# Cross-attention on one core: GpSimd's input split and output scale-and-shift cut into single instructions, with other work between the halves

## The chip, the cores and the metric

The kernel runs on one core of one Trainium2 chip. A time is device microseconds (us) of one execution. Five engines each work through a list of their own: TensorE (PE: matmuls), VectorE (DVE), ScalarE (ACT), GpSimd (POOL) and SyncE (SP), which here issues nearly all DMAs. They meet only at semaphores.

## The reference

```python
Q = (q @ Wq + bq); K = (k @ Wk + bk); V = (v @ Wv + bv)     # q = x, k = v = ctx; 16 heads of 64
scores = einsum('bhqd,bhkd->bhqk', Q, K) / 8 * mask
ctx = einsum('bhqk,bhkd->bhqd', softmax(scores), V)
x = q + ctx @ Wo + bo
return (x - mean(x)) * rsqrt(var(x) + 1e-5) * gamma + beta
```

The batch has 16 items, each with 512 queries, 512 keys and width 512; all is float32.

## The kernel before

Each float32 operand of a large matmul is carried as two float16 parts, a rounded one and the difference that is left ("split"), so that a product takes three matmuls. ScalarE rounds, and VectorE takes the difference, for Q, K, V, the probabilities and the context; for the inputs x and ctx it is GpSimd that takes it. All differences of probabilities are VectorE's already (`split_probs`, L933), in both kernels.

A batch item has 8 pairs of heads. A pair has 4 query tiles of 128 rows and two heads, so 8 score tiles of 128x512. A tile goes: TensorE `scores` (L436) into one of 4 PSUM banks; VectorE `mask_and_max` (L919) masks and takes the row maxima; GpSimd `negate_max` (L1228) negates the maxima of two tiles; ScalarE `exponentials` (L608) writes `probs` and frees the bank; GpSimd `scale_sums` (L1234) scales the row sums of four tiles; VectorE `invert_sums` (L927) inverts them; ScalarE `round_probs` (L622) and VectorE `split_probs` (L933) make the two parts; SP issues a transposing DMA (L275), and TensorE `values` (L457) multiplies by V. `probs` has 8 buffers, so an exponential waits for the `split_probs` of the same tile of the pair before.

The projections ("fills", L383 to L385) and the output projection share three PSUM banks. After the output projection of item n: VectorE adds (L962) and takes statistics, GpSimd `deviation` (L1244 to L1252) makes the scale and shift of the layer norm, ScalarE `standardize` (L638) applies them, and GpSimd `scale_and_shift` multiplies by gamma (L1258) and adds beta (L1260) for each of four row tiles of 128x512. Each second instruction waits for the first. SP `store` (L265) waits for the result.

For the next item, ScalarE `round_input` (L576) rounds a 128x512 tile of x or ctx; then GpSimd `split_input` scales the raw tile (L1208) and subtracts the rounded part (L1211). The Q fill of the next item waits for all four tiles of x, its K fill for all four of ctx.

Each engine's `body(prev, here, nxt, first)` is an order written out by hand for a software pipeline over batch items: `here` is the item whose pairs 2 to 7 run, `nxt` the item whose inputs are prepared and whose pairs 0, 1 and a part of 2 start at the end of the body, and `prev` the one whose output is normalized. `batches` calls it once with only `nxt`, once for item 0, then in a hardware loop for items 1 to 14 (a "pass" below), and twice to finish. In a list an instruction that waits holds back all that is behind it. SP's list at the end of a body has: transpose of pair 0's query tile 0 of `nxt`, `store` of `prev`'s tiles 0 to 2, load of `acc` tile 0, transpose of query tile 1, `store` of tile 3.

Of the kernel before, what the change touches and what calls it, by code (L numbers as in the profile page):

```python
# [41 lines left out]
def cross_attention(nc, x, xt, ct, mask, wq, bq, wk, bk, wv, bv, wo, bo, gamma, beta, out):  # L42
    ctx = ExitStack()
    with ctx:
# [142 lines left out]
        def out_no(n, q):  # L187
            return n * QT + q + 1
# [17 lines left out]
        def raw_input(t, i):  # L206
            return raw[:, "xc".index(t), i, :]
# [988 lines left out]
        def _(pool):  # L1196
# [27 lines left out]
            def negate_max(n, p, queries):  # L1224
                for q in queries:
                    wait_alone(pool, masked, tile_no(n, p, 2 * q + 1))
                    cut = slice(2 * q, 2 * q + 2)
                    nc.gpsimd.tensor_scalar(neg_max[:, p % 2, cut], row_max[:, p % 2, cut], -1.0, 1.0, ALU.mult,  # L1228
                                            ALU.mult).then_inc(max_negated, 1)
# [21 lines left out]
                pool.wait_ge(rstd_done, n + 1)  # L1251
                nc.gpsimd.tensor_tensor(shift, neg_mean, rstd, ALU.mult).then_inc(shift_done, 1)  # L1252

            def scale_and_shift(n, tiles):
                for q in tiles:
                    i = out_no(n, q)
                    pool.wait_ge(centered, i)
                    nc.gpsimd.tensor_tensor(acc[:, q, :], acc[:, q, :], gamma_b[:, :], ALU.mult).then_inc(scaled, 1)  # L1258
                    pool.wait_ge(scaled, i)
                    nc.gpsimd.tensor_tensor(acc[:, q, :], acc[:, q, :], beta_b[:, :], ALU.add).then_inc(normed, 1)  # L1260

            def body(prev, here, nxt, first):
                if here is not None:
                    scale_sums(here, 2, 0)
                if prev is not None:
                    add_bo(prev, range(1, 2))
                if here is not None:
                    negate_max(here, 2, range(2, 4))
                    scale_sums(here, 2, 1)
                    negate_max(here, 3, range(0, 2))  # L1270
                    scale_sums(here, 3, 0)
                if prev is not None:
                    add_bo(prev, range(2, 4))
                if here is not None:
# [12 lines left out]
                if prev is not None:  # L1287
                    scale_and_shift(prev, range(0, 1))
                if here is not None:
                    negate_max(here, 5, range(2, 4))  # L1290
                    scale_sums(here, 5, 1)
                if nxt is not None:
                    split_input(nxt, "x", range(0, 1))
                if here is not None:
                    negate_max(here, 6, range(0, 1))
                if nxt is not None:
                    split_input(nxt, "x", range(1, 2))
                    scale_biases(nxt)
                if here is not None:
                    negate_max(here, 6, range(1, 2))  # L1300
                if nxt is not None:
                    split_input(nxt, "x", range(2, 3))
                if here is not None:
                    scale_sums(here, 6, 0)
                    negate_max(here, 6, range(2, 3))
                if nxt is not None:
                    split_input(nxt, "x", range(3, 4))
                if here is not None:
                    negate_max(here, 6, range(3, 4))
                if nxt is not None:  # L1310
                    split_input(nxt, "c", range(0, 1))
                if here is not None:
                    scale_sums(here, 6, 1)
                if nxt is not None:
                    split_input(nxt, "c", range(1, 2))
                if here is not None:
                    negate_max(here, 7, range(0, 2))
                if nxt is not None:
                    split_input(nxt, "c", range(2, 4))
                if here is not None:  # L1320
                    scale_sums(here, 7, 0)
                    negate_max(here, 7, range(2, 4))
                    scale_sums(here, 7, 1)
                if prev is not None:
                    scale_and_shift(prev, range(1, 3))
                if nxt is not None:
                    negate_max(nxt, 0, range(0, 2))
                    scale_sums(nxt, 0, 0)
                    negate_max(nxt, 0, range(2, 4))
                    scale_sums(nxt, 0, 1)  # L1330
                    negate_max(nxt, 1, range(0, 1))
                if prev is not None:
                    scale_and_shift(prev, range(3, 4))
                if nxt is not None:
                    negate_max(nxt, 1, range(1, 2))
                    scale_sums(nxt, 1, 0)
                    negate_max(nxt, 1, range(2, 4))
# [33 lines left out]
```

## Time and profile before

| | us |
|---|---|
| median of 3 runs | 2435.55 (2431.52 to 2437.57) |
| profiled execution, its own time | 2432.53 |
| its span, first to last instruction | 2430.7 |
| PE busy | 2206.0 (91%) |
| DVE busy | 2099.9 (86%) |
| ACT busy | 1790.6 (74%) |
| POOL busy | 824.3 (34%) |

A pass of the hardware loop takes about 146.5 us; the rows below are of one of them (here = item 6; VectorE branches back at 968 us and at 1115 us), and the others repeat it closely. Busy shares are averages, so what counts is who waits for whom in each stretch.

### The profile page before, as it was taken

The page shows a single profiled execution, that of the slowest core. Times are in us where ns is not written, and L with a number is a line of the kernel's source. Part 1 is how long each engine was busy: PE and PEld are TensorE (multiplying, and loading weights), DVE is VectorE, ACT ScalarE, POOL GpSimd, SP SyncE. Part 2 cuts the span into 40 slices and gives each one's busy share as a digit, 9 for nine tenths or more (in the row PEclk, how much of TensorE's full clock was granted, in tenths as well). Part 3 has the DMA queues.
Part 4 walks back from the last instruction along what each step waited for, and adds up shares of the span by engine and source line. Part 5 has one row for each costly group of instructions (what it writes and reads, how often), then busy time and mean ns, then how long its engine had stood idle before and what let it go on. Part 6 is the DMA issues. An engine that isn't in the chain of part 4 may idle for free.

```text
span 2430.7 us, 45821 instructions
## 1 busy us (share of the span) xinstructions
PE 2206.0 (91%) x12348; PEld 897.6 (37%) x12348; DVE 2099.9 (86%) x4411; ACT 1790.6 (74%) x3809; POOL 824.3 (34%) x1320
## 2 busy tenths in 40 slices
PE   3789999999999899999989999999999999999995
PEld 1234433334333343333334333343333334333342
DVE  6799988979889898888989889798888979889893
ACT  3688786867868687786877858687786867859782
POOL 2023252423425243242423415143242422415324
PEclk9899999999999999999999999999999999999997
DMA  5378887677767868677687777868677687767774
GB/s 203 74 149 158 164 148 160 130 169 144 159 143 148 179 125 179 133 146 166 130 172 144 155 148 147 172 127 177 135 143 169 125 175 143 151 141 148 158 134 109
DMA packets 1117592, 363.26 MB, mean 149 GB/s; under 512 B 1073504, under 2 KB 1073504, under 8 KB 1117408
## 3 DMA queue, kind: packets, MB, share of 16 engines
q1 hardware_dynamic: 1114288, 361.58, 72.7%
q14 instruction: 165, 1.35, 0.2%
q10 hardware_dynamic: 3120, 0.01, 0.1%
q8 instruction: 19, 0.31, 0.0%
HBM read 76.30 MB, written 16.78 MB: 38 GB/s over the span
## 4 chain that ended last, share of the span: by engine, by line
PE 51%; issue 16%; ACT 11%; DVE 11%; POOL 8%; DMA 1%; DVEq 1%; ACTq 1%; POOLq 0%; SPq 0%
PE fill_ps L383 12%; PE fill_ps L384 11%; PE fill_ps L385 11%; PE score_ps L436 9%; PE ctx_ps L457 6%; ACT probs L608 5%; DVE p L933 4%; DVE score_ps L919 3%; ACT p L622 2%; POOL acc L1258 2%; ACT v L587 2%; POOL raw L1208 2%; POOL neg_max L1228 2%; POOL acc L1260 1%; DVE row_max L919 1%
## 5 line engine op out<-in xcount | busy, mean ns | idle before, releaser
L608 ACT ACTIVATE probs<-score_ps,neg_max 128x512 f32<-128x512 f32 x1024 | 694.4, 685 | 312.4 <-POOL neg_max L1228 272.2
L933 DVE SCALAR_TENSOR_TENSOR p<-probs,inv_sum,p 128x512 f16<-128x512 f32 x1024 | 851.8, 872 | 1.8 <-ACT p L622 1.8
L919 DVE CUSTOM_DVE_ANT_0 score_ps<-score_ps,mask_sb,small 128x512 f32<-128x512 f32 x1024 | 728.1, 751 | 46.6 <-PE score_ps L436 41.0
L622 ACT ACTIVATE p<-probs,inv_sum 128x512 f16<-128x512 f32 x1024 | 681.8, 724 | 79.4 <-DVE inv_sum L927 75.9
L436 PE MATMUL score_ps<-k,q 64*128 64x512 f16 x3072 | 457.1, 389 | 106.0 <-ACT probs L608 104.0
L1228 POOL TENSOR_SCALAR neg_max<-row_max 128x2 f32<-128x2 f32 x512 | 176.6, 346 | 1040.3 <-DVE row_max L919 1039.0
L457 PE MATMUL ctx_ps<-pT,v 128*64 128x512 f16 x3072 | 361.3, 385 | 17.9 <-DMA pT<-p 11.8
L436 PEld LDWEIGHTS score_ps<-k,q 64*128 64x128 f16 x3072 | 139.1, 95 | 397.4 <-ACT probs L608 240.5
L457 PEld LDWEIGHTS ctx_ps<-pT,v 128*64 128x64 f16 x3072 | 166.3, 111 | 207.0 <-issue 63.4
L383 PE MATMUL fill_ps<-cT,wk 128*128 128x512 f16 x512 | 202.7, 396 | 26.0 <-DVE k L948 24.9
L1234 POOL TENSOR_SCALAR down_sum<-row_sum 128x4 f32<-128x4 f32 x256 | 75.3, 294 | 398.3 <-ACT probs L608 390.6
L383 PE MATMUL fill_ps<-wv,cT 128*128 128x512 f16 x512 | 199.7, 390 | 6.5 <-DVE v L954 6.5
L608 ACT ACTIVATION_READ_ACCUMULATOR probs<-score_ps,neg_max 128x1 f32 x1024 | 205.2, 200 | 0.0
L383 PE MATMUL fill_ps<-xT,wq 128*128 128x512 f16 x512 | 196.9, 385 | 5.2 <-POOL xT L1211 5.2
L384 PE MATMUL fill_ps<-cT,wk 128*128 128x512 f16 x512 | 201.0, 393 | 0.0
L385 PE MATMUL fill_ps<-cT,wk 128*128 128x512 f16 x512 | 199.3, 389 | 0.0
L384 PE MATMUL fill_ps<-wv,cT 128*128 128x512 f16 x512 | 198.0, 387 | 0.0
L385 PE MATMUL fill_ps<-wv,cT 128*128 128x512 f16 x512 | 197.3, 385 | 0.0
L384 PE MATMUL fill_ps<-xT,wq 128*128 128x512 f16 x512 | 196.3, 383 | 0.0
L385 PE MATMUL fill_ps<-xT,wq 128*128 128x512 f16 x512 | 196.2, 383 | 0.0
L862 DVE TENSOR_REDUCE small<-raw 128x1 f32<-128x512 f32 x128 | 85.0, 676 | 127.6 <-issue 122.5
L383 PE MATMUL fill_ps<-wo,ctx 128*128 128x512 f16 x512 | 194.5, 380 | 0.0
(89 smaller groups left out, 2839.1 us busy)
## 6 DMA issues: line engine op xcount, KB each, us to landing
raw<-in_xt SPq DMA_DIRECT2D x64, 256.0 KB, 4.0
raw<-in_ct SPq DMA_DIRECT2D x64, 256.0 KB, 3.4
mask_sb<-in_mask_Bx1xSxS_fk SPq DMA_DIRECT2D x64, 256.0 KB, 3.0
acc<-in_x SPq DMA_DIRECT2D x64, 256.0 KB, 3.2
out<-acc SPq DMA_DIRECT2D x64, 256.0 KB, 2.5
pT<-p SPq DMA_TRANSPOSE x512, 4.6
wq_staged<-in_L_xattn_Wq SPq DMA_DIRECT2D x4, 512.0 KB, 7.1
wk_staged<-in_L_xattn_Wk SPq DMA_DIRECT2D x4, 512.0 KB, 11.0
```

The source lines that it names most:

```text
L383: nc.tensor.matmul(bank, lhs[0], rhs[0], start=is_start, stop=False)
L384: nc.tensor.matmul(bank, lhs[1], rhs[0], start=False, stop=False)
L385: return nc.tensor.matmul(bank, lhs[0], rhs[1], start=False, stop=is_last)
L436: mm = nc.tensor.matmul(banks[a], qk16["q"][halves[a], par, lq, cut], qk16["k"][halves[a], par, lk, :], start=lq == lk, stop=lk == 1)
L457: mm = nc.tensor.matmul(ctx_ps[a * DH:(a + 1) * DH, :], v16[:, g % 1, t, piece, col:col + DH], pT[:, par, :, a, plane, t, :], start=t == 0 ...
L608: nc.scalar.activation(probs[:, i % E_TILES, :], score_ps[:, i % 4, :], ACT.Exp, bias=neg_max[:, p % 2, i:i + 1], accum_out=row_sum[:, p % ...
L622: nc.scalar.activation(p16[:, q, a, 0, :], probs[:, i % E_TILES, :], ACT.Copy, scale=inv_sum[:, p % 2, i:i + 1]).then_inc(p_rounded, 1)
L862: nc.vector.tensor_reduce(xc_max[t][:, i:i + 1], raw_input(t, i), AXIS.X, ALU.max, apply_absolute_value=True).then_inc(xc_max_taken[t], 1)
L919: nc.vector.tensor_tensor_reduce(out=score_ps[:, i % 4, :], in0=score_ps[:, i % 4, :], in1=mask_sb[:, q, :], scale=score_scale, scalar=-3. ...
L933: nc.vector.scalar_tensor_tensor(out=p16[:, q, a, 1, :], in0=probs[:, i % E_TILES, :], scalar=inv_sum[:, p % 2, i:i + 1], in1=p16[:, q, a, ...
L1228: nc.gpsimd.tensor_scalar(neg_max[:, p % 2, cut], row_max[:, p % 2, cut], -1.0, 1.0, ALU.mult, ALU.mult).then_inc(max_negated, 1)
L1234: nc.gpsimd.tensor_scalar(down_sum[:, p % 2, cut], row_sum[:, p % 2, cut], P_DOWN, 1.0, ALU.mult, ALU.mult).then_inc(sum_scaled, 1)
```

## The change

`split_input` becomes `scale_input` and `split_input`, `scale_and_shift` becomes `scale_out` and `shift_out`. The instructions and their shapes, numbers and waits stay; only GpSimd's order changes: `negate_max` and `scale_sums` of pairs 6 and 7 now stand between the scaling and the subtraction of an input tile; beta of output tile 0 goes from pair 5 to after `negate_max` of pair 7; beta of tiles 1 and 2 goes from before to after `negate_max` and `scale_sums` of pair 0 of the next item; beta of tile 3 goes to after `scale_sums(nxt, 1, 0)`. No other engine's list changes.

```diff
-            def split_input(n, t, tiles):
+            def scale_input(n, t, tiles):
                 c = "xc".index(t)
                 for i in tiles:
                     wait_alone(pool, xc_rounded[t], n * DT + i + 1)
                     wait_alone(pool, xc_max_taken[t], n * DT + i + 1)
                     nc.gpsimd.tensor_scalar(raw_input(t, i), ...).then_inc(xc_scaled[t], 1)
+
+            def split_input(n, t, tiles):
+                for i in tiles:
                     wait_alone(pool, xc_scaled[t], n * DT + i + 1)
                     nc.gpsimd.tensor_tensor(xc16[t][:, i, 1, :], ...).then_inc(xc_split[t], 1)
@@
-            def scale_and_shift(n, tiles):
+            def scale_out(n, tiles):
                 for q in tiles:
                     i = out_no(n, q)
                     pool.wait_ge(centered, i)
                     nc.gpsimd.tensor_tensor(acc[:, q, :], acc[:, q, :], gamma_b[:, :], ALU.mult).then_inc(scaled, 1)
+
+            def shift_out(n, tiles):
+                for q in tiles:
+                    i = out_no(n, q)
                     pool.wait_ge(scaled, i)
                     nc.gpsimd.tensor_tensor(acc[:, q, :], acc[:, q, :], beta_b[:, :], ALU.add).then_inc(normed, 1)
```

GpSimd's order in a pass, from pair 5 on (n: `negate_max`, s: `scale_sums`, with pair and query tile or half; the items prev, here, nxt as in the code):

```
before
 prev gamma0 beta0 | n5.2 n5.3 s5.1 | x0 scale x0 split | n6.0 | x1 scale x1 split biases | n6.1
 x2 scale x2 split | s6.0 n6.2 | x3 scale x3 split | n6.3 | c0 scale c0 split | s6.1
 c1 scale c1 split | n7.0 n7.1 | c2 scale c2 split c3 scale c3 split | s7.0 n7.2 n7.3 s7.1
 prev gamma1 beta1 gamma2 beta2 | nxt n0.0 n0.1 s0.0 n0.2 n0.3 s0.1 n1.0 | prev gamma3 beta3
 nxt n1.1 s1.0 n1.2 n1.3 ...
after
 prev gamma0 | n5.2 n5.3 s5.1 | x0 scale | n6.0 | x0 split x1 scale biases | n6.1
 x1 split x2 scale | s6.0 n6.2 | x2 split x3 scale | n6.3 | x3 split c0 scale | s6.1
 c0 split c1 scale | n7.0 | c1 split | n7.1 | c2 scale c2 split c3 scale c3 split | s7.0 n7.2 n7.3
 prev beta0 | s7.1 | prev gamma1 gamma2 | nxt n0.0 n0.1 s0.0 n0.2 n0.3 s0.1
 prev beta1 beta2 | nxt n1.0 | prev gamma3 | nxt n1.1 s1.0 | prev beta3 | nxt n1.2 n1.3 ...
```

## Rows read from the trace of the kernel before

**Rows 1.** The page: busy time, share of the span and instructions of each engine.

```profile
PE 2206.0 (91%) x12348; PEld 897.6 (37%) x12348; DVE 2099.9 (86%) x4411; ACT 1790.6 (74%) x3809; POOL 824.3 (34%) x1320
```

**Rows 2.** Stretches of a pass: length, busy PE, PEld, DVE, ACT, POOL; clock, DMA, GB/s.

```profile
978.00:1053.00 75.00, 71.86 (x409) 29.74 (x410) 73.78 (x163) 56.65 (x123) 25.08 (x44) 1.00 0.71 137
1053.00:1085.70 32.70, 29.45 (x182) 11.64 (x180) 28.35 (x55) 27.15 (x57) 17.09 (x22) 0.98 0.71 143
831.50:978.00 146.50, 136.99 (x770) 55.36 (x770) 129.15 (x272) 110.61 (x236) 51.66 (x82) 0.98 0.74 151
```

**Rows 3.** Waits over the span: engine, line waited for, us, times, longest.

```profile
ACT probs L608 <- POOL neg_max L1228: 272.2, 240, 4.6
...
DVE small L862 <- issue: 122.5, 14, 10.2
```

**Rows 4.** GpSimd in order of time: start, us, instruction, [idle before and its releaser].

```profile
1029.53 1.27 POOL L1260 TENSOR_TENSOR acc<-acc,beta_b 128x512 f32<-128x512 f32 x1
...
1055.35 0.69 POOL L1208 TENSOR_SCALAR raw<-raw,small 128x512 f32<-128x512 f32 x1 [3.62 <-ACT cT L576]
1056.23 1.16 POOL L1211 TENSOR_TENSOR cT<-raw,cT 128x512 f16<-128x512 f32 x1 [0.18 <-POOL raw L1208]
1057.47 0.20 POOL L1234 TENSOR_SCALAR down_sum<-row_sum 128x4 f32<-128x4 f32 x1
...
1075.24 1.28 POOL L1258 TENSOR_TENSOR acc<-acc,gamma_b 128x512 f32<-128x512 f32 x1
...
1079.19 1.60 POOL L1260 TENSOR_TENSOR acc<-acc,beta_b 128x512 f32<-128x512 f32 x1
1080.76 1.29 POOL L1228 TENSOR_SCALAR neg_max<-row_max 128x2 f32<-128x2 f32 x2
```

**Rows 5.** VectorE in order of time.

```profile
1053.22 0.75 DVE L954 SCALAR_TENSOR_TENSOR v<-fill_ps,small,v 128x512 f16<-128x512 f32 x1 [0.74 <-ACT v L587]
1054.47 0.75 DVE L954 SCALAR_TENSOR_TENSOR v<-fill_ps,small,v 128x512 f16<-128x512 f32 x1 [0.50 <-ACT v L587]
...
1057.70 0.18 DVE L927 RECIPROCAL inv_sum<-down_sum 128x4 f32<-128x4 f32 x1 [1.75 <-POOL down_sum L1234]
...
1076.78 0.75 DVE L919 CUSTOM_DVE_ANT_0 score_ps<-score_ps,mask_sb,small 128x512 f32<-128x512 f32 x1
...
1084.71 0.18 DVE L927 RECIPROCAL inv_sum<-down_sum 128x4 f32<-128x4 f32 x1 [1.39 <-POOL down_sum L1234]
...
1093.02 0.76 DVE L919 CUSTOM_DVE_ANT_0 score_ps<-score_ps,mask_sb,small 128x512 f32<-128x512 f32 x1 [1.96 <-PE score_ps L436]
```

**Rows 6.** ScalarE in order of time.

```profile
1040.90 0.69 ACT L608 ACTIVATE probs<-score_ps,neg_max 128x512 f32<-128x512 f32 x1 [1.00 <-POOL neg_max L1228]
...
1075.12 3.19 ACT L622 ACTIVATE p<-probs,inv_sum 128x512 f16<-128x512 f32 x5
1081.50 0.69 ACT L608 ACTIVATE probs<-score_ps,neg_max 128x512 f32<-128x512 f32 x1 [3.19 <-POOL neg_max L1228]
```

**Rows 7.** A stretch of TensorE: length, busy; granted clock, DMA, GB/s.

```profile
1082.30:1087.80 5.50, 4.90 (x17) 0.69 1.20 193
```

**Rows 8.** `split_probs` in four windows: min/median/max ns, first and last start.

```profile
L933 DVE SCALAR_TENSOR_TENSOR p<-probs,inv_sum,p x1: 1783/1783/1783, 1029.6 to 1029.6; 128x512 f16<-128x512 f32 x1
...
L933 DVE SCALAR_TENSOR_TENSOR p<-probs,inv_sum,p x6: 739/824/1672, 1041.1 to 1047.8; 128x512 f16<-128x512 f32 x6
...
L933 DVE SCALAR_TENSOR_TENSOR p<-probs,inv_sum,p x4: 1152/1404/1641, 1060.8 to 1064.5; 128x512 f16<-128x512 f32 x4
...
L933 DVE SCALAR_TENSOR_TENSOR p<-probs,inv_sum,p x5: 739/739/1758, 1078.8 to 1082.6; 128x512 f16<-128x512 f32 x5
```

**Rows 9.** `mask_and_max` over the span: min/median/max ns.

```profile
L919 DVE CUSTOM_DVE_ANT_0 score_ps<-score_ps,mask_sb,small x1024: 723/753/768, 52.8 to 2372.4; 128x512 f32<-128x512 f32 x171
```

**Rows 10.** TensorE in order of time, just behind the branch.

```profile
979.22 0.39 PE L383 MATMUL fill_ps<-cT,wk 128*128 128x512 f16 x1 [1.96 <-DVE k L948]
```

**Rows 11.** The page: `split_probs`, busy us, mean ns of one, idle before.

```profile
L933 DVE SCALAR_TENSOR_TENSOR p<-probs,inv_sum,p 128x512 f16<-128x512 f32 x1024 | 851.8, 872 | 1.8 <-ACT p L622 1.8
```

More of the change, by code:

```diff
@@ L1287, in body @@
                 if prev is not None:
-                    scale_and_shift(prev, range(0, 1))
+                    scale_out(prev, range(0, 1))
                 if here is not None:
@@ L1292, in body @@
                 if nxt is not None:
-                    split_input(nxt, "x", range(0, 1))
+                    scale_input(nxt, "x", range(0, 1))
                 if here is not None:
@@ L1296, in body @@
                 if nxt is not None:
-                    split_input(nxt, "x", range(1, 2))
+                    split_input(nxt, "x", range(0, 1))
+                    scale_input(nxt, "x", range(1, 2))
                     scale_biases(nxt)
@@ L1301, in body @@
                 if nxt is not None:
-                    split_input(nxt, "x", range(2, 3))
+                    split_input(nxt, "x", range(1, 2))
+                    scale_input(nxt, "x", range(2, 3))
                 if here is not None:
@@ L1306, in body @@
                 if nxt is not None:
-                    split_input(nxt, "x", range(3, 4))
+                    split_input(nxt, "x", range(2, 3))
+                    scale_input(nxt, "x", range(3, 4))
                 if here is not None:
@@ L1310, in body @@
                 if nxt is not None:
-                    split_input(nxt, "c", range(0, 1))
+                    split_input(nxt, "x", range(3, 4))
+                    scale_input(nxt, "c", range(0, 1))
                 if here is not None:
@@ L1314, in body @@
                 if nxt is not None:
+                    split_input(nxt, "c", range(0, 1))
+                    scale_input(nxt, "c", range(1, 2))
+                if here is not None:
+                    negate_max(here, 7, range(0, 1))
+                if nxt is not None:
                     split_input(nxt, "c", range(1, 2))
                 if here is not None:
-                    negate_max(here, 7, range(0, 2))
+                    negate_max(here, 7, range(1, 2))
                 if nxt is not None:
-                    split_input(nxt, "c", range(2, 4))
+                    scale_input(nxt, "c", range(2, 3))
+                    split_input(nxt, "c", range(2, 3))
+                    scale_input(nxt, "c", range(3, 4))
+                    split_input(nxt, "c", range(3, 4))
                 if here is not None:
@@ L1322, in body @@
                     negate_max(here, 7, range(2, 4))
+                if prev is not None:
+                    shift_out(prev, range(0, 1))
+                if here is not None:
                     scale_sums(here, 7, 1)
                 if prev is not None:
-                    scale_and_shift(prev, range(1, 3))
+                    scale_out(prev, range(1, 3))
                 if nxt is not None:
@@ L1330, in body @@
                     scale_sums(nxt, 0, 1)
+                if prev is not None:
+                    shift_out(prev, range(1, 3))
+                if nxt is not None:
                     negate_max(nxt, 1, range(0, 1))
                 if prev is not None:
-                    scale_and_shift(prev, range(3, 4))
+                    scale_out(prev, range(3, 4))
                 if nxt is not None:
@@ L1336, in body @@
                     scale_sums(nxt, 1, 0)
+                if prev is not None:
+                    shift_out(prev, range(3, 4))
+                if nxt is not None:
                     negate_max(nxt, 1, range(2, 4))
```

## The prediction

> **What bounds the kernel now.** First the page's engine line: TensorE is busy 91% and VectorE 86% of the span [rows 1]. Neither share says where a pass loses time, so next comes the view by stretches of one pass [rows 2]. From 978 to 1053 VectorE is busy 73.8 of 75 us: it sets the pace there. From 1053 to 1085.7 it is busy 28.35 of 32.7 us, and TensorE 29.45: both wait. Then the waits: ScalarE's exponentials waited 272 us in all for the negated maxima that GpSimd writes, and VectorE loses 122.5 us in 14 waits of which the profile shows no cause [rows 3]; these 8.75 us stand where the loop branches back, once in a pass, and the change doesn't touch them. Last the order in time. GpSimd is busy 34% [rows 1], but it is in the way at the wrong moment: it multiplies and adds for output tiles 1 and 2 from 1075.24 to 1080.79 and only then negates the maxima of pair 0 [rows 4], though VectorE had them at 1077.6 (1076.78 + 0.75, and a short read of the result) [rows 5]. ScalarE had nothing else to do after 1078.31 (1075.12 + 3.19) and idled 3.19 us until its exponential at 1081.50 [rows 6]. That wait passes on: the scores wait for the bank, VectorE waits 1.39 us for the row sums and 1.96 us for scores [rows 5], and TensorE, after a gap, runs 5.5 us at a granted clock of 0.69, a mixture of its two levels, 2.4 and 1.2 GHz [rows 7].
>
> **The change part by part.** Nothing is added or removed: GpSimd issues as many instructions as before, in another order. I count on VectorE's list, whose end closes a pass, in us gained per pass. What I call s0.0 and the like are the names of the order shown above.
>
> (a) Beta of tile 0 leaves 1029.53 [rows 4]. A probability split that starts beside it takes 1783 ns; an undisturbed one takes 739 (the minimum of rows 8), so 1.04 goes. Its new place, after n7.3, is free until s7.1, but it meets a split of pair 7 there: between 0 and 1.04 comes back; I take 0.5, the middle. Net 0.5 (0 to 1.0).
>
> (b) n6.0 and n6.1 go in front of the subtractions of x0 and x1. Now n6.0 comes behind x0's, and ScalarE waited 1.00 for it [rows 6]. That this wait goes gains nothing by itself where VectorE sets the pace. What VectorE gains is that fewer of its splits lie beside a subtraction: of the six from 1041.1 to 1047.8 the longest has 1672, with a median of 824 [rows 8]. One long split less gains 0.9, two 1.9; a new one costs 0.9. I take 0.7 (-0.9 to 1.9), near one less.
>
> (c) VectorE's waits for V, 0.74 and 0.50 [rows 5], stand because the last V fills end late, behind pair 6's scores, which wait for ScalarE. If those go, TensorE comes sooner. Of 1.24 I take 0.7 (0 to 1.24).
>
> (d) s6.1 now stands in front of c0's subtraction. Its exponentials had ended; yet it ran at 1057.47 behind the 1.16 us subtraction of 1056.23 [rows 4], and VectorE waited 1.75 for it [rows 5]. It still stands behind c0's scaling at 1055.35, which waits for ScalarE's rounding [rows 4], so 0.8 of the wait stays: 0.95 (0.5 to 1.75). The next four splits, 1152 to 1641 ns [rows 8], stay beside the work on ctx: nothing.
>
> (e) The main part. Beta 1 and 2 move behind s0.1. GpSimd then has two products of 1.28 from 1075.24 [rows 4], done at 1077.9; n0.0 follows at once, its maxima being there, and the exponential starts when ScalarE is free, at 1078.4 in place of 1081.50: 3.1 us earlier. TensorE's next scores find their banks free when its values end, at 1081.0, and have no gap. VectorE behind it: of the five splits from 1078.8 one is 1758 long beside the second beta [rows 8], so 1.0 goes; the wait of 1.39 goes, since s0.0 is there at about 1081.7, before the splits end at 1082.2; of the 1.96 for scores I take 1.7, as TensorE also gains the clock: 31% of 5.5 us [rows 7] is 1.7. Sum 4.1 (2.0, if the wait for scores stays and the clock still falls, to 4.5).
>
> What is late next: the two betas stand in front of n1.0. They end 2.9 us after s0.1; the maxima for n1.0 come 2.1 us after it (an inversion, two masks of 0.75 and hand-overs), so GpSimd is 0.8 late. ScalarE has five roundings and one normalization before it needs n1.0, 5 x 0.64 (3.19 / 5, rows 6) and more than that, so it is covered; without this cover it would cost 0.8.
>
> (f) Gamma 3 alone stands in front of n1.1, where it was gamma and beta; it lies beside splits as beta did. Beta 3, behind s1.0, lies beside `mask_and_max`, whose 1024 instructions all take 723 to 768 ns whatever GpSimd does [rows 9]. Gain 0.3 (-0.7 to 1.0: one long split more or less).
>
> (g) SP's list. `store` of tiles 0 to 2 now waits for beta 2, 2.9 us after s0.1, with the load of acc tile 0 and the transpose of pair 0's query tile 1 behind it. That transpose needs a split that VectorE reaches only after an inversion, four masks and one split, 4 us and more, so it isn't late. `store` of tile 3 waits for beta 3, with the transpose of query tile 2 behind it: I find that up to 2 us later against its split than before, and only a rounding in the next pass wants it: 0 (-0.5 to 0).
>
> Sum of a pass: 0.5 + 0.7 + 0.7 + 0.95 + 4.1 + 0.3 = 7.25. I hold back 0.55 for waits that take the place of these, as VectorE reaches everything sooner: 6.7. There are 14 passes with prev, here and nxt: 93.8. The call for item 0 has nxt but no prev, so (b) to (d): 2.3. The last two calls have no nxt, so none waits behind the output work: 0. Together 96. Against the profiled execution's own 2432.5: 2336.5. The runs' median is 3.0 above that execution: 2339.5, said as 2340.
>
> A rule that speaks against this change. A split that meets a 128x512 GpSimd instruction takes 1152 to 1783 ns instead of 739 [rows 8], and `mask_and_max`, with one operand in PSUM, keeps its time [rows 9]. The Trainium skill, page "GPSIMD Engine Reference", section "1. Specifications", says that GpSimd's SBUF interfaces are shared with VectorE, with contention for VectorE instructions that have two SBUF inputs. The rows agree. By it the change removes no contention and only gives GpSimd's instructions other neighbours; its result is the slower rival below.
>
> **The rivals.** *TensorE becomes the bound.* It is busy 137.0 of 146.5 us [rows 2] and idles about 4 behind VectorE's branch (1.96 before a fill [rows 10] and as much before scores). That leaves 5.5 a pass: 14 x 5.5 = 77, so 2358. For it: TensorE has hardly a gap from 978 to 1037. Against it: 1.7 us of the busy time is the slow clock of rows 7. *Only half pays.* VectorE is never idle from 978 to 1053, so its splits may meet GpSimd as often as before and (a) to (d) give nothing; (e) and (f) less what I hold back are 3.85 x 14 = 54: 2382. *No change.* The exponentials come early, but something that these rows don't show closes the pass, such as the DMAs for the transposes: 2435, within 7. *Slower.* The shared interface decides. A split has a mean of 872 ns [rows 11] against 739, so 64 of them lose 8.5 us a pass, about nine meetings of 0.93 (1672 less 739). GpSimd has 20 large instructions with two inputs in a pass. If each comes to lie on a split, that is 18.6, so 10.1 more than now, against 4.8 us of waits saved in (c), (d) and (e): 5.3 slower x 14 = 74, 2510. It decides from the point where more than five further instructions meet a split. Against it: betas 1, 2 and 3 go where VectorE has masks.
>
> **How the numbers follow.** Forecast (6 to 8.7 us a pass) 60%, TensorE the bound 15%, half 15%, no change 5%, slower 5%. The range goes down to 8.7 a pass, 122 us, so 2315: all upper ends together, 11.4, would need every split undisturbed at once. Upwards it takes in the half case and a little more, 2.6 a pass, so 36 and 2400. Faster by over 0.3% (7 us, about what a measurement of this kernel tells from none) holds the first three cases, 0.90; within it 0.05; slower 0.05.
>
> **What the profile after would show.** (a) the split beside the evacuation of K in pair 6 back at 0.74. (b) ScalarE's 1.00 before pair 6's first exponential gone. (d) VectorE's wait before the inversion of pair 6's second half at 0.8 or less. (e) ScalarE's 3.19 under 0.5, VectorE's 1.39 and 1.96 gone, a granted clock of 1.00 from pair 0's scores on. The whole: passes of about 139.8 us. I am wrong if those waits go and the pass stays above 143, which would be TensorE or the transposes, or if the mean of `split_probs` rises above 872 ns, which would be the shared interface.

## The result and the profile after

The changed kernel takes 2307.39 us in the median (2306.32 to 2312.85, 4 runs) against 2434.33 for the kernel before (2431.52 to 2437.57): ratio 0.9483, 95% interval 0.9463 to 0.9502. That is 127 us less where 96 were forecast: the forecast was 2340, and the time lies below its range of 2315 to 2400. A pass of the loop, from VectorE's branch to its next in the trace, has a mean of 137.6 us instead of 146.3, so 8.7 us less and not 6.7.

The page of the changed kernel, busy times of the engines and the groups of the exponentials and of the splits; it answers to [rows 1, 3, 11].

```profile
PE 2153.6 (93%) x12348; PEld 889.5 (38%) x12348; DVE 2003.8 (87%) x4411; ACT 1783.7 (77%) x3809; POOL 825.6 (36%) x1320
...
L608 ACT ACTIVATE probs<-score_ps,neg_max 128x512 f32<-128x512 f32 x1024 | 693.1, 684 | 177.3 <-POOL neg_max L1231 174.4
...
L933 DVE SCALAR_TENSOR_TENSOR p<-probs,inv_sum,p 128x512 f16<-128x512 f32 x1024 | 757.8, 781 | 5.1 <-ACT p L622 5.1
```

VectorE lost 96 us of busy time without losing one instruction: a split has a mean of 781 ns instead of 872. The exponentials waited 174 us for GpSimd instead of 272.

The stretches of one pass (VectorE branches at 651.0 and at 788.2 us; 661 here answers to 978 there), columns as in [rows 2].

```profile
661.00:736.00 75.00, 73.26 (x425) 30.40 (x426) 73.02 (x166) 59.46 (x130) 24.61 (x44) 1.00 0.72 137
736.00:763.00 27.00, 27.00 (x175) 11.45 (x174) 24.82 (x56) 25.99 (x53) 15.61 (x21) 1.00 0.82 161
651.00:788.20 137.20, 132.64 (x772) 54.75 (x771) 122.20 (x272) 110.10 (x236) 51.86 (x82) 0.99 0.78 161
```

From 736 to 763 TensorE is now busy all the 27 us; before it had gaps there. Over the pass VectorE is busy 122.2 us instead of 129.2, and TensorE 132.6 instead of 137.0.

GpSimd in order of time, answering to [rows 4].

```profile
735.66 0.69 POOL L1208 TENSOR_SCALAR raw<-raw,small 128x512 f32<-128x512 f32 x1 [3.04 <-ACT cT L576]
736.44 0.20 POOL L1237 TENSOR_SCALAR down_sum<-row_sum 128x4 f32<-128x4 f32 x1
736.72 1.16 POOL L1214 TENSOR_TENSOR cT<-raw,cT 128x512 f16<-128x512 f32 x1
...
750.96 1.28 POOL L1267 TENSOR_TENSOR acc<-acc,beta_b 128x512 f32<-128x512 f32 x1
...
753.59 2.51 POOL L1261 TENSOR_TENSOR acc<-acc,gamma_b 128x512 f32<-128x512 f32 x2
756.36 0.19 POOL L1231 TENSOR_SCALAR neg_max<-row_max 128x2 f32<-128x2 f32 x1 [0.27 <-DVE row_max L919]
```

The row sums of pair 6 (L1237, 736.44) stand in front of c0's subtraction, beta of tile 0 (L1267) lies behind pair 7's last maxima, and pair 0's maxima at 756.36 follow two products (L1261). VectorE in the same stretches, answering to [rows 5, 8]:

```profile
712.57 0.72 DVE L933 SCALAR_TENSOR_TENSOR p<-probs,inv_sum,p 128x512 f16<-128x512 f32 x1
...
733.35 0.75 DVE L954 SCALAR_TENSOR_TENSOR v<-fill_ps,small,v 128x512 f16<-128x512 f32 x1 [0.18 <-ACT v L587]
734.78 0.75 DVE L954 SCALAR_TENSOR_TENSOR v<-fill_ps,small,v 128x512 f16<-128x512 f32 x1 [0.69 <-ACT v L587]
...
736.67 0.18 DVE L927 RECIPROCAL inv_sum<-down_sum 128x4 f32<-128x4 f32 x1 [0.41 <-POOL down_sum L1237]
...
744.47 0.76 DVE L919 CUSTOM_DVE_ANT_0 score_ps<-score_ps,mask_sb,small 128x512 f32<-128x512 f32 x1 [1.66 <-PE score_ps L436]
...
767.36 0.76 DVE L919 CUSTOM_DVE_ANT_0 score_ps<-score_ps,mask_sb,small 128x512 f32<-128x512 f32 x1 [0.52 <-PE score_ps L436]
```
```profile
L933 DVE SCALAR_TENSOR_TENSOR p<-probs,inv_sum,p x5: 740/752/793, 724.5 to 732.4; 128x512 f16<-128x512 f32 x5
```
```profile
L933 DVE SCALAR_TENSOR_TENSOR p<-probs,inv_sum,p x3: 744/745/1096, 740.4 to 741.7; 128x512 f16<-128x512 f32 x3
```

The split that beta of tile 0 had met (1783 in [rows 8]) is back at 0.72 (712.57). The two waits for V, 0.74 and 0.50 before, are 0.18 and 0.69. The wait for s6.1 went from 1.75 to 0.41, the one before s0.0's inversion (1.39) is gone, and the one for pair 1's scores went from 1.96 to 0.52. A new one of 1.66, for scores of pair 7, stands at 744.47. The five splits before 737, those of pair 5 among them, are all at 793 ns or less, and of the four of pair 6, 1152 to 1641 before, the window shows three, with a median of 745 and one of 1096; the fourth, the first of the run at 739.73, took 742.

ScalarE around pair 0's first exponential, answering to [rows 6]; that stretch's busy times and granted clock, to [rows 7]; and TensorE behind the branch, to [rows 10].

```profile
753.46 3.33 ACT L622 ACTIVATE p<-probs,inv_sum 128x512 f16<-128x512 f32 x5
756.69 0.67 ACT L608 ACTIVATE probs<-score_ps,neg_max 128x512 f32<-128x512 f32 x1
```
```profile
759.50:765.00 5.50, 5.50 (x35) 2.32 (x32) 5.50 (x14) 4.87 (x12) 0.63 (x3) 1.00 1.17 195
```
```profile
655.03 2.80 PE L436 MATMUL score_ps<-k,q 64*128 64x512 f16 x11 [2.68 <-ACT probs L608]
...
662.23 0.39 PE L383 MATMUL fill_ps<-cT,wk 128*128 128x512 f16 x1 [1.37 <-DVE k L948]
```

ScalarE goes from its roundings to the exponential with no wait, where it had 3.19 us, and the granted clock of the 5.5 us of pair 0's scores and the fill behind them is 1.00 (the third number from the end). TensorE's two waits behind the branch, 2.68 and 1.37 here, are together what they were (2.06, seen in the same view of before, and 1.96 in [rows 10]), and they are all that is left: from 667 to 760 it is busy 92.5 of 93 us.

### The profile page after: what moved, and what is told of

It is laid out like the page before. It is cut to its first block, busy times and chain, and to the rows that moved or that the text cites. A ratio compares the mean times of both kernels' runs of the same rounds, so it can differ in the third digit from the quotient of the medians.

```text
span 2311.1 us, 45821 instructions
## 1 busy us (share of the span) xinstructions
PE 2153.6 (93%) x12348; PEld 889.5 (38%) x12348; DVE 2003.8 (87%) x4411; ACT 1783.7 (77%) x3809; POOL 825.6 (36%) x1320
## 4 chain that ended last, share of the span: by engine, by line
PE 81%; issue 8%; DVE 7%; ACT 2%; POOL 1%; DMA 1%; DVEq 0%; SPq 0%; ACTq 0%; POOLq 0%
PE fill_ps L383 18%; PE fill_ps L384 17%; PE fill_ps L385 17%; PE score_ps L436 15%; PE ctx_ps L457 13%; DVE score_ps L919 2%; DVE p L933 2%; ACT probs L608 1%; DVE k L948 0%; DMA pT<-p 0%; DVE small L801 0%; PE ctx_ps L370 0%; ACT p L622 0%; DMA wq_staged<-in_L_xattn_Wq 0%; DVE row_max L919 0%
## 5 line engine op out<-in xcount | busy, mean ns | idle before, releaser
L933 DVE SCALAR_TENSOR_TENSOR p<-probs,inv_sum,p 128x512 f16<-128x512 f32 x1024 | 757.8, 781 | 5.1 <-ACT p L622 5.1
L1231 POOL TENSOR_SCALAR neg_max<-row_max 128x2 f32<-128x2 f32 x512 | 170.1, 332 | 977.1 <-DVE row_max L919 974.6
L436 PE MATMUL score_ps<-k,q 64*128 64x512 f16 x3072 | 416.9, 387 | 50.1 <-ACT probs L608 44.5
L436 PEld LDWEIGHTS score_ps<-k,q 64*128 64x128 f16 x3072 | 133.5, 95 | 308.4 <-ACT probs L608 122.8
L1237 POOL TENSOR_SCALAR down_sum<-row_sum 128x4 f32<-128x4 f32 x256 | 79.1, 309 | 379.5 <-ACT probs L608 371.9
L383 PE MATMUL fill_ps<-cT,wk 128*128 128x512 f16 x512 | 197.0, 385 | 17.5 <-DVE k L948 16.4
L384 PE MATMUL fill_ps<-cT,wk 128*128 128x512 f16 x512 | 196.0, 383 | 0.0
L385 PE MATMUL fill_ps<-cT,wk 128*128 128x512 f16 x512 | 195.8, 382 | 0.0
```

What stands on the lines that cost most here:

```text
L383: nc.tensor.matmul(bank, lhs[0], rhs[0], start=is_start, stop=False)
L384: nc.tensor.matmul(bank, lhs[1], rhs[0], start=False, stop=False)
L385: return nc.tensor.matmul(bank, lhs[0], rhs[1], start=False, stop=is_last)
L436: mm = nc.tensor.matmul(banks[a], qk16["q"][halves[a], par, lq, cut], qk16["k"][halves[a], par, lk, :], start=lq == lk, stop=lk == 1)
L933: nc.vector.scalar_tensor_tensor(out=p16[:, q, a, 1, :], in0=probs[:, i % E_TILES, :], scalar=inv_sum[:, p % 2, i:i + 1], in1=p16[:, q, a, ...
L1237: nc.gpsimd.tensor_scalar(down_sum[:, p % 2, cut], row_sum[:, p % 2, cut], P_DOWN, 1.0, ALU.mult, ALU.mult).then_inc(sum_scaled, 1)
```

## The experiments

All ratios are to the kernel before on the same chip. "Pass" is the mean of 13 passes of the profiled execution, measured as above; "split" is the mean of `split_probs` on the page (872 before). The ratios carry the argument. The pass column sets single executions on different chips against each other: the profiled one before took 2432.5 us, while the medians of the kernel before on the other chips are 2427.0 to 2432.7, so differences to 146.3 can be too large by up to 0.4 us.

| kernel | ratio (95%) | pass us | split ns |
|---|---|---|---|
| before | 1 | 146.3 | 872 |
| changed | 0.9483 (0.9463 to 0.9502) | 137.6 | 781 |
| input half alone | 0.9729 (0.9712 to 0.9747) | 141.0 | 813 |
| output half alone | 0.9709 (0.9691 to 0.9728) | 140.6 | 831 |
| old order, short stand-ins | 0.9598 (0.9582 to 0.9615) | 138.6 | 757 |
| new order, short stand-ins | 0.9483 (0.9467 to 0.9499) | 137.1 | 757 |
| old order, long stand-ins | 0.9810 (0.9786 to 0.9834) | 142.3 | 760 |
| new order, long stand-ins | 0.9492 (0.9477 to 0.9508) | 137.3 | 758 |
| changed, less TensorE work | 0.9419 (0.9396 to 0.9442) | 136.5 | 788 |
| changed, less VectorE work | 0.9417 (0.9395 to 0.9440) | 136.3 | 733 |
| changed, four more additions | 0.9587 (0.9566 to 0.9609) | 138.9 | 808 |
| changed, ctx order back | 0.9598 (0.9583 to 0.9613) | 139.3 | 810 |
| changed, x order back | 0.9572 (0.9557 to 0.9586) | 138.7 | 805 |
| changed, bo added earlier | 0.9490 (0.9477 to 0.9503) | 137.5 | 768 |
| only beta 0 moved | 0.9937 (0.9918 to 0.9955) | 144.4 | 858 |
| only beta 1, 2 moved | 0.9813 (0.9791 to 0.9835) | 142.5 | 860 |
| only x interleaved | 0.9859 (0.9838 to 0.9880) | 143.7 | 846 |
| only ctx interleaved | 0.9803 (0.9782 to 0.9824) | 142.2 | 840 |

**The two halves.** The edits are the parts of the change itself; in each the other half is as before.

> Only the input half of the change: scale_input and split_input interleaved with pairs 6 and 7, each beta right behind its gamma as before. Theory C (most of the gain is that VectorE's probability splits no longer lie beside GpSimd's large instructions; 4.5 us a pass of that stretch came from scalings and subtractions of x and ctx): 2365 to 2380 us. Theory W (the gain is waits for GpSimd that go, as the prediction's sum has it; (b) to (d) are 2.35 a pass): 2395 to 2405.

> Only the output half: gamma and beta cut apart and moved, each input tile scaled and subtracted in one go as before. Theory C: 3.4 us a pass of stretch on the splits came from gammas and betas, with the waits behind them 4 to 5 a pass: 2365 to 2378. Theory W: (a), (e), (f) are 4.9 a pass: 2366. The two theories part on the sum of this run's gain and the other half's: C wants 127 us or more in all (each half also hides what the other leaves), W about 101.

2.7% and 2.9%: together 5.6%, 137 us, where the whole has 5.2%, 127. So the halves share some 10 us that either gains alone. By its ratio the input half is worth 4.4 us a pass (0.0271 x 2427 / 15), nearly twice the 2.35 that the prediction gave it; the output half comes out at 5.0 (0.0291 x 2427 / 14), where its terms had 4.9. By the pass column they are 5.3 and 5.7. Scaled to the first chip, the halves take 2368 and 2363 us: theory C has the right size for the inputs (theory W wanted 2395 or more), and both fit the outputs within 3 us.

**Order and interface apart.** GpSimd's large instructions are replaced by powers of a few columns, which keep it busy but hardly touch SBUF. The order and the waits stay.

```diff
+            def raise_ones(out_ap, cols_):
+                return nc.gpsimd.tensor_tensor(out_ap, ones[:, 0:cols_], half4[:, 0:cols_], ALU.pow)
 ...
-                    nc.gpsimd.tensor_tensor(acc[:, q, :], acc[:, q, :], gamma_b[:, :], ALU.mult).then_inc(scaled, 1)
+                    raise_ones(acc[:, q, 0:4], 4).then_inc(scaled, 1)
 ...
```

> The order of the kernel before. Left out: from item 1 on the 128x512 scalings and subtractions of the inputs, and all 128x512 gammas and betas, are replaced by a power of 2 or 4 columns that keeps GpSimd about as long (about 1 us for 4 columns) and hardly touches SBUF. GpSimd is in the way as long as before, but no split can be stretched by it. Theory C: some 7.5 us a pass of stretch goes and the waits stay, 2320 to 2345 us. Theory W: the waits remain and only little changes, 2410 or more.

> The changed kernel with the same replacement (the same work left out). What is left of stretch there is 1.2 us a pass without the one beside the addition of bo, which stays. Theory C: the difference to the kernel before with the replacement is only the waits, at most 3 us a pass, so 2280 to 2300, and the change is worth 20 to 40 us here and not 127. Theory W: the change is worth as much as with the real instructions, 100 or more. If TensorE is the bound after the change: 2295 to 2307.

This looked like the proof of theory C: 98 us gained without any change of order, and only 28 left for the order. But the page showed the gamma and beta stand-ins with a mean of 1057 ns, shorter than the 1.28 to 1.60 us of the real ones, and two pairs of them lie in front of pair 0's maxima. So they were made longer, 6 columns for gamma and beta and 5 for the subtractions (4 before), with exponents from another small tile:

> The order of the kernel before, with the same work left out as in the run of the old order with small powers, but powers of 6 columns for gamma and beta and of 5 for the subtractions, so that GpSimd is in the way at least as long as with the real ones (there 1.04 us stood for 1.28 to 1.60). Theory C (shared interface): still within 10 us of 2329 scaled to this chip, since the shorter stand-ins were not what gained. Theory W (time in GpSimd's list before the maxima): the 0.24 to 0.5 us on each of 8 instructions come back, up to 4 us a pass: 2370 or more.

> The changed kernel's order with the long stand-ins (6 columns for gamma and beta, 5 for the subtractions; the same work left out as in the old order with long stand-ins, which took 0.981 of the kernel before, 142.3 us a pass). This closes the square of order and interface. If the order alone, without any stretch, is worth about the 4.75 us a pass of waits that the prediction counted: 137 to 138 us a pass, 0.947 to 0.951. If the order is worth little without the interface: 0.970 or more. If the stand-ins of 1.3 to 1.4 us are themselves too long for the new order: 0.955 to 0.965.

The groups of GpSimd's stand-ins for gamma and beta in the old order, and the splits on that page.

```profile
L1204 POOL TENSOR_TENSOR acc<-ones,small 128x6 f32<-128x6 f32 x128 | 178.4, 1398 | 10.3 <-ACT acc L638 2.9
```
```profile
L933 DVE SCALAR_TENSOR_TENSOR p<-probs,inv_sum,p 128x512 f16<-128x512 f32 x1024 | 737.6, 760 | 24.2 <-ACT p L622 24.0
```

Longer stand-ins, a mean of 1398 ns instead of 1057 on the 8 of gamma and beta and of 1281 to 1364 instead of 1100 to 1120 on the 8 of the subtractions, cost 2.1% of the time (0.9810 less 0.9598), 52 us; which of the two groups cost how much is not separated. Theory C as I had put it falls, as it wanted the time within 10 us of the short ones. Theory W had this run right (2370 or more; measured 2384), but it can't explain the 46 us that are gained all the same with GpSimd busy as long as before. Read as a square with long stand-ins: in the old order the interface alone is worth 1.9% (46 us, 4.0 a pass by the pass lengths), and with the interface quiet the order alone is worth 0.9810 to 0.9492, 3.2% (77 us, 5.0 a pass). In the new order the interface is worth nothing that can be measured (0.9492 and 0.9483 against 0.9483). The two shares hold for this way through the square, interface first: taken the other way, with the real instructions in place, the new order gains all 5.2% and making the interface quiet adds nothing. A pair of gamma and beta is 2.80 us with the long stand-ins and 2.71 by the means of 1281 and 1430 in the kernel before, so the 1.9% is if anything too low and the 3.2% too high.

**What bounds the changed kernel.** One matmul of each Q and K fill left out; or the split of each pair's last tile cut to 128 columns.

```diff
-                nc.tensor.matmul(bank, lhs[1], rhs[0], start=False, stop=False)
+                if not drop:        # drop: kind in "QK" and j == parts - 1
+                    nc.tensor.matmul(bank, lhs[1], rhs[0], start=False, stop=False)
```
```diff
+                    c = slice(0, 128) if i == 7 and not is_first(n) else slice(0, S)
-                        out=p16[:, q, a, 1, :], in0=probs[:, i % E_TILES, :], ...
+                        out=p16[:, q, a, 1, c], in0=probs[:, i % E_TILES, c], ...
```

> The changed kernel with one matmul of 128x512 left out of each Q and K fill (the last second product), 16 a pass, 16 x 0.216 = 3.46 us of TensorE. If TensorE is the bound of the changed kernel: 2.4 to 3.5 us less a pass, 35 to 50 us below the changed kernel. If VectorE still is: within 10 us of it.

> The changed kernel with the split of each pair's last tile cut from 512 to 128 columns from item 1 on (the rest of it left out), 8 a pass, about 8 x 0.45 = 3.6 us of VectorE. If TensorE is the bound of the changed kernel: within 10 us of it. If VectorE is: 35 to 50 us below it. If both are at the limit: 10 to 25 in this and in the run with less of TensorE.

Both give 16 us (2307 x (1 - 0.9419 / 0.9483)), 1.1 and 1.3 a pass, of 3.46 removed on TensorE and 3.1 on VectorE (64 x 48 ns by the means). Neither engine is the bound alone: of a saving on either, some two thirds don't reach the time. That they take turns within a pass fits this; the stretches in which each leads were not told apart.

**More meetings.** Four additions of 128x512 into a spare tile where GpSimd is idle:

```diff
+                    extra(here, range(0, 2))       # nc.gpsimd.tensor_tensor(pad[:, k % 2, :], gamma_b, beta_b, ALU.add)
                     negate_max(here, 3, range(0, 2))
```

> The changed kernel with four more 128x512 additions a pass on GpSimd into a spare tile, two behind the row sums of pair 2 and two between the maxima of pair 4, where GpSimd is idle for 4 to 6 us and VectorE has splits. Theory C: each meets a split, 2 to 3.7 us more of stretch a pass; if VectorE has no slack there, 28 to 50 us slower than the changed kernel, if TensorE covers for it 10 to 25. Theory W: GpSimd has the time, within 5 us.

The mean of a split rose from 781 to 808, so 64 x 27 ns = 1.7 us a pass, and the time by 1.1%, 25 us; a pass of the profiled execution is 1.3 us longer. VectorE's busy time rose by 28 us (2003.8 to 2031.8). Theory W, within 5 us, fails here. The waits of the exponentials for GpSimd's maxima rose too, from 174 to 197 us in all, so that a part of the 25 may be maxima that came later; the run doesn't separate it.

**The inputs' order back, one at a time, and bo earlier.**

```diff
 # ctx back                                           # x back
-scale_input c0 | scale_sums 6.1 | split_input c0      -scale_input x0 | negate_max 6.0 | split_input x0
+scale_input c0 | split_input c0 | scale_sums 6.1      +scale_input x0 | split_input x0 | negate_max 6.0
 ...                                                   ...
```
```diff
-                    negate_max(nxt, 1, range(2, 4))
+                    negate_max(nxt, 1, range(2, 3))
                 if here is not None:
                     add_bo(here, range(0, 1))
                 if nxt is not None:
+                    negate_max(nxt, 1, range(3, 4))
                     negate_max(nxt, 2, range(0, 2))
```

> The changed kernel with the four ctx tiles scaled and subtracted in one go as before (the row sums of pair 6 again behind c0's subtraction, pair 7's first maxima behind c1's). By the prediction's (d) this gives 0.95 us a pass back: 0.953 to 0.955 of the kernel before. By theory C the four splits of pair 6 are stretched again, 2 to 2.6 more: 0.960 to 0.966, unless TensorE, which holds VectorE back 1.66 us just behind them, covers it: then 0.949 to 0.953.

> The changed kernel with the four x tiles scaled and subtracted in one go as before; ctx stays interleaved. By the prediction's (b) and (c), 1.4 us a pass back: 0.956 to 0.958 of the kernel before. By theory C the three stretched splits of pair 5, 2.0 us, return: 0.960 or more. If covered by TensorE's fills: 0.949 to 0.953.

> The changed kernel with the addition of bo to output tile 0 one place earlier, behind the third instead of the fourth maxima of pair 1 of the next item, where VectorE has masks and evacuations from PSUM. It meets a split of 1.75 now, in every pass. Theory C with VectorE at the limit: up to 1.0 us a pass less, 0.943 to 0.946. If TensorE takes half, as the runs with less work on either engine say: 0.945 to 0.947. If the addition now waits for its load or delays the maxima: 0.949 or more.

ctx's order gives 1.2% back, 1.9 us a pass over 15: at the lower edge of what theory C had, and twice the 0.95 of the prediction's (d). x's gives 0.9% back, 1.4 a pass, as (b) and (c) had. The earlier addition of bo was a try to beat the changed kernel, and it didn't: the split that took 1750 ns in every pass is free, but the time is the same within the intervals. The same evacuation of V, in order of time on VectorE, first in the changed kernel and then with bo earlier:

```profile
778.78 3.75 DVE L933 SCALAR_TENSOR_TENSOR p<-probs,inv_sum,p 128x512 f16<-128x512 f32 x4
783.27 0.75 DVE L954 SCALAR_TENSOR_TENSOR v<-fill_ps,small,v 128x512 f16<-128x512 f32 x1 [0.74 <-ACT v L587]
```
```profile
1053.27 0.14 DVE L919 DVE_READ_ACCUMULATOR2_ANT row_max<- 128x1 f32 x1
...
1057.76 0.75 DVE L954 SCALAR_TENSOR_TENSOR v<-fill_ps,small,v 128x512 f16<-128x512 f32 x1 [1.75 <-ACT v L587]
```

The four splits take 2.73 instead of 3.75, and the wait behind them 1.75 instead of 0.74: it is the V fill of TensorE that ends there.

**Each term alone, on the kernel before.** Each is the one part of the change named, on an otherwise unchanged order.

> The kernel before with only beta of tile 0 moved, behind pair 7's last maxima: the prediction's (a) alone. By its sum 0.5 us a pass: 0.997 of the kernel before (7 us). If the split that met it is simply free and nothing else is met: 1.0 us, 0.994. If more waits open than close: 1.000.

> The kernel before with only the betas of tiles 1 and 2 moved, behind the row sums of pair 0 of the next item: the prediction's (e) alone. By its sum 4.1 us a pass: 0.976 of the kernel before. The whole output half gave 0.9709, which leaves 0.7 us a pass for (a) and (f) if (e) was right. If (e) was too small by the missing part: 0.972. If it was too large, because VectorE's splits take up the waits: 0.980 or more.

> The kernel before with only the x tiles interleaved: (b) and (c) alone. By the prediction 1.4 us a pass: 0.992. If the three stretched splits of pair 5 and the wait behind the V fills all go, 2.0 and 1.2: 0.982 to 0.985.

> The kernel before with only the ctx tiles interleaved: (d) alone. By the prediction 0.95 us a pass: 0.995. If the four splits of 1152 to 1641 ns are free as well, 2.6 more: 0.980 to 0.985, less what TensorE holds back behind them (1.66 in the changed kernel).

In us over a whole run (1% is 24.3) and a pass (over 14, the inputs over 15): (a) 15, 1.1; (e) 45, 3.2; (b) with (c) 34, 2.3; (d) 48, 3.2. For (f) the output half less (a) and (e) leaves 10, 0.7. The sum is 152, of which the whole has 127.

One thing that they share can be seen. VectorE's wait of 1.96 before pair 1's scores [rows 5], which the prediction put under (e), isn't there in every pass of the kernel before. TensorE's first matmul of pair 0's scores in the pass of [rows 7] and in another pass of the same execution, and for the latter the stretch and the wait:

```profile
1082.33 0.39 PE L436 MATMUL score_ps<-k,q 64*128 64x512 f16 x1 [1.27 <-ACT probs L608]
```
```profile
791.43 0.39 PE L436 MATMUL score_ps<-k,q 64*128 64x512 f16 x1 [1.24 <-ACT probs L608]
```
```profile
791.40:796.90 5.50, 4.91 (x25) 1.88 (x26) 4.05 (x11) 5.05 (x12) 0.39 (x2) 1.00 1.25 193
```
```profile
800.48 0.76 DVE L919 CUSTOM_DVE_ANT_0 score_ps<-score_ps,mask_sb,small 128x512 f32<-128x512 f32 x1 [0.33 <-PE score_ps L436]
```

There TensorE had waited 1.24 us before pair 0's scores, nearly as long as the 1.27 in the pass of [rows 7]; yet its granted clock over the 5.5 us from there stayed at 1.00 instead of falling to 0.69, VectorE's wait was 0.33, and the pass took 144.9 us.

| kernel | TensorE's gap | passes with the clock at 1.00, of 12 | VectorE's wait in them | in the others | mean |
|---|---|---|---|---|---|
| before | 1.24 to 1.27 | 2 | 0.33 | 1.67 to 1.97 | 1.65 |
| (a) alone | 1.15 | 10 | 0.33 to 0.34 | 1.81 to 1.92 | 0.59 |
| (b), (c) alone | 1.22 to 1.24 | 11 | 0.33 to 0.34 | 1.98 | 0.47 |
| (d) alone | 0.57 to 0.60 | 12 | 0.33 to 0.34 | | 0.33 |
| (e) alone | none | 12 | 0.42 to 0.43 | | 0.43 |
| changed | none | 12 | 0.51 to 0.53 | | 0.52 |

In the other passes the clock over these 5.5 us is 0.69 to 0.74. So each part alone gains 1.1 to 1.3 us a pass at this wait, and the whole gains 1.1 once. The four together exceed the whole by 3.7 a pass here, twice the 25 us that are to be explained; so either the parts help one another elsewhere, or the one profiled execution of each isn't typical (that of (a) was the fastest of its six runs, 2407 against a median of 2412). Stretch and wait with only ctx interleaved:

```profile
1065.90:1071.40 5.50, 4.80 (x25) 1.79 (x26) 4.04 (x11) 5.05 (x13) 0.39 (x2) 1.00 1.25 198
```
```profile
1075.09 0.76 DVE L919 CUSTOM_DVE_ANT_0 score_ps<-score_ps,mask_sb,small 128x512 f32<-128x512 f32 x1 [0.33 <-PE score_ps L436]
```

The four splits of pair 6 and GpSimd beside them in the kernel before:

```profile
1060.68 0.69 POOL L1208 TENSOR_SCALAR raw<-raw,small 128x512 f32<-128x512 f32 x1
1061.56 1.37 POOL L1211 TENSOR_TENSOR cT<-raw,cT 128x512 f16<-128x512 f32 x1 [0.18 <-POOL raw L1208]
1062.91 1.12 POOL L1208 TENSOR_SCALAR raw<-raw,small 128x512 f32<-128x512 f32 x1
1064.22 1.37 POOL L1211 TENSOR_TENSOR cT<-raw,cT 128x512 f16<-128x512 f32 x1 [0.18 <-POOL raw L1208]
```
```profile
1060.76 5.37 DVE L933 SCALAR_TENSOR_TENSOR p<-probs,inv_sum,p 128x512 f16<-128x512 f32 x4
```

The kernel before with only ctx interleaved: the same four splits, GpSimd beside them, and VectorE before and behind them.

```profile
L933 DVE SCALAR_TENSOR_TENSOR p<-probs,inv_sum,p x4: 745/747/1098, 1045.7 to 1047.7; 128x512 f16<-128x512 f32 x4
```
```profile
1042.45 0.20 POOL L1237 TENSOR_SCALAR down_sum<-row_sum 128x4 f32<-128x4 f32 x1
...
1044.75 1.16 POOL L1214 TENSOR_TENSOR cT<-raw,cT 128x512 f16<-128x512 f32 x1
1045.88 0.66 POOL L1231 TENSOR_SCALAR neg_max<-row_max 128x2 f32<-128x2 f32 x1
1046.52 1.77 POOL L1208 TENSOR_SCALAR raw<-raw,small 128x512 f32<-128x512 f32 x1
1048.47 1.37 POOL L1214 TENSOR_TENSOR cT<-raw,cT 128x512 f16<-128x512 f32 x1 [0.18 <-POOL raw L1208]
1049.83 0.70 POOL L1208 TENSOR_SCALAR raw<-raw,small 128x512 f32<-128x512 f32 x1
1050.71 1.16 POOL L1214 TENSOR_TENSOR cT<-raw,cT 128x512 f16<-128x512 f32 x1 [0.18 <-POOL raw L1208]
```
```profile
1042.69 0.18 DVE L927 RECIPROCAL inv_sum<-down_sum 128x4 f32<-128x4 f32 x1 [0.41 <-POOL down_sum L1237]
...
1045.74 3.08 DVE L933 SCALAR_TENSOR_TENSOR p<-probs,inv_sum,p 128x512 f16<-128x512 f32 x4
1050.17 0.76 DVE L919 CUSTOM_DVE_ANT_0 score_ps<-score_ps,mask_sb,small 128x512 f32<-128x512 f32 x1 [1.34 <-PE score_ps L436]
```

The wait before the inversion is 1.34 us shorter (1.75 to 0.41), where (d) took 0.95. With that the splits start at 1045.74 while c1's subtraction ends and only a small `negate_max` follows. Now it is GpSimd's next scaling that comes second: it takes 1.77 us instead of 0.69. Before, a scaling began at 1060.68 just ahead of the first split at 1060.76, and from there the two engines alternated. VectorE's run of four splits went from 5.37 us to 3.08, 2.3 less, while GpSimd's two scalings and two subtractions of c2 and c3 went from 4.55 in sum to 5.00. So most of the stretch is gone and only a little went over to GpSimd.

Who starts first decides, as a count over the trace of the kernel before shows. Of GpSimd's 128x512 sums and products, the 58 that began while no split ran and then met one took 1.15 to 1.28 us, as long as the 169 that met none; the 93 that began while a split ran took 1.36 to 1.78. The other way round, the 16 splits that were already running when such an instruction began, and met no other, took 0.74 to 0.75; one that began just behind it took up to 1.79.

## Why the prediction was wrong

**The step that failed is (d)**, in its words "The next four splits, 1152 to 1641 ns, stay beside the work on ctx: nothing". I took GpSimd's and VectorE's lists to keep their phase. Moving s6.1 and n7.0 shifted the one against the other by a us or two, the run of splits got to the interface first, and 2.3 us of stretch went. Alone (d) measured 3.2 us a pass and not 0.95, and taken out of the changed kernel 1.9. The alone figure is made up of 2.3 of stretch, 1.34 of the wait for s6.1, 1.3 at the wait for pair 1's scores, and a new wait of 1.34 for scores of pair 7 against them, 3.6 in sum. The mechanism was named and priced in the text (for the slower rival), but used only where I saw an instruction leave its place.

The same shows over the whole pass. From before to after, the splits of a pass lost 6.6 us of time over 742 ns each (9.0 to 2.4, the mean of 12 passes), where my terms had about 2.5 (0.5, 0.7, 1.0 and 0.3). The waits gained less than the 4.7 that I gave them: VectorE's for row sums fell from 3.1 to 0.4, but those for scores rose from 1.65 to 2.6, since 1.66 for scores of pair 7 is new. The 0.55 held back for new waits was too little. Not all the stretch was worth its time: by the square, nearly all of it together is worth 4.0 us a pass in the old order.

(a) 1.1 measured, 0.5 predicted: above 0.5 partly by luck, since 1.1 us a pass of its profiled execution is the wait for pair 1's scores, of which (a) says nothing. (b) and (c) 2.3 against 1.4: the long splits of pair 5 went altogether (the longest was 1672 in [rows 8] and is 793 in the changed kernel), 1.2 came from the same wait for scores, and of the 1.24 of waits for V only 0.4 went, not 0.7. (e) 3.2 alone against 4.1. Its steps all show: no wait for 3.19, no 1.39, 0.52 for 1.96, a clock of 1.00. But the last wait was 1.65 in the mean and not 1.96, 0.43 of it stays, and any other part gains it as well. (f) about 0.7 against 0.3, by difference only. (g) holds: SP's later stores cost nothing that shows.

Of the rivals, TensorE as the bound came half true. It has no waits left but those behind the branch, as that case had it; but the pass is 137.6 and not 141, because the 137.0 us of busy time that I took as fixed fell to 132.6 itself, and VectorE limits as much as TensorE does. The granted clock of the pass rose from 0.98 to 0.99, which is about 1.4 of the 4.4 us; the rest isn't explained. The half case, the one without change and the slower one are out. The slower rival's mechanism is real: four more additions cost 25 us. Its direction was wrong here. The Trainium skill's page "GPSIMD Engine Reference", section "1. Specifications", says that GpSimd's SBUF interfaces are shared with VectorE, with contention where a VectorE instruction has two SBUF inputs. The traces agree: a split met by GpSimd took up to 1.79 us instead of 0.74, and `mask_and_max`, with one input in PSUM, stayed at 0.72 to 0.77.

By the two signs that I had given for being wrong, the pass is not above 143 and the mean of the splits is not above 872; I had given none for the gain being larger.

What stays open: why the clock falls in ten of twelve passes of the kernel before and not in the other two, after the same gap; why the parts exceed the whole by only 25 us, when the shared wait for scores alone comes to twice that; and what the 25 us of the four added additions are made of.

## What to carry to other kernels

When two engines share an interface, a stretched instruction in the trace is a meeting, and here its price fell on the one that came second; a change of order moves the phase of all meetings behind it, so count every stretched instruction downstream as free or kept, and give both ends to the range. Look at the same wait in several passes before you price it: one pass showed 1.96 where the mean was 1.65, and each of four parts alone removed most of it. A long instruction pair on a slow engine in front of a tiny one that others wait for should be cut, even where that engine is two thirds idle. And stand-ins that are 0.1 to 0.3 us shorter than what they replace can produce a false cause: keep the length when you take away the traffic.

## What the runs showed of the hardware

- A `split_probs` of 128x512 with both inputs in SBUF took 0.74 us alone and up to 1.79 when it began behind one of GpSimd's two-input instructions. The other way round, GpSimd's one-input scaling took 0.69 us alone and 1.77 when it began within a run of four back-to-back splits. `mask_and_max`, with one input in PSUM, took 0.72 to 0.77 in every run.
- At one place of the loop TensorE stood idle for 1.24 to 1.27 us in every pass of the kernel before. Over the next 5.5 us its granted clock was 0.69 to 0.74, between its two levels of 1.2 and 2.4 GHz, in ten passes of twelve and 1.00 in two. The ten took 145.9 to 147.3 us and the two 144.3 and 144.9.
- GpSimd's power of 6 columns took 1.40 us and of 4 columns 1.06, near the 1.15 to 1.28 of an undisturbed sum or product of 512 columns: stand-ins of a given length are easy to build.
